# Keys of a cross-attention kernel from seven products of block sums instead of eight

## The chip, the cores and the metric

One core of one Trainium2 chip. The metric is the device time of one execution in microseconds; the times shown are medians over runs of the same kernel. TensorE is called PE here, its weight load PEld, VectorE DVE, ScalarE ACT, GpSimd POOL, and SyncE's DMA queue SP.

## The reference, cut to what matters

A first attention (1x1 convolutions `theta`, `phi` and `g`, a product without softmax, a convolution back, batch norm, residual) turns x [8, 256, 512], with ctx [8, 256, 512], into the rows that enter two layers of cross-attention with 16 heads of 128, and an MLP. Both layers take keys and values from the same context:

```python
def _cross_attention(q_in, kv_in, wq, bq, wk, bk, wv, bv, wo, bo, bias_k, bias_v):
    qh = (q_in @ wq + bq).reshape(b, q_len, H, K)
    kh = (kv_in @ wk + bk).reshape(b, t, H, K)
    vh = (kv_in @ wv + bv).reshape(b, t, H, K)
    kh = jnp.concatenate([kh, jnp.broadcast_to(bias_k, (b, 1, H, K))], axis=1)
    vh = jnp.concatenate([vh, jnp.broadcast_to(bias_v, (b, 1, H, K))], axis=1)
    logits = jnp.einsum('bqhk,bthk->bhqt', qh, kh) / scale
    weights = jax.nn.softmax(logits, axis=-1)
    ctx = jnp.einsum('bhqt,bthk->bqhk', weights, vh).reshape(b, q_len, H * K)
    return ctx @ wo + bo
```

The change concerns `kv_in @ wk`: 2048 context tokens by 512 features, times 512 by 2048 weights, for each of two layers.

## The kernel before, in words

Every large product is made of two parts. An operand is split into a high part (rounded to fp32r) and a low part (what the rounding left), and `product` issues three matmuls for each chunk of 128 features: high by high, high by low, low by high. A high part is one copy or activation, a low part is one subtraction: ACT and DVE make them for activations, POOL for weights (`halve`: a cast, then a subtraction that waits for it).

The front of the kernel computes all keys and values and stores them to DRAM (`kd`, `vd`); behind it, 64 steps load them back, do the attention, and the MLP follows. The front has 8 groups (`GROUPS`), each of four heads. A group has 16 key units (one head by one chunk of 512 tokens, 12 matmuls of 512 columns: 4 chunks of features, 3 each) and 16 value units (one tile of 128 tokens by four heads, 12 matmuls too). The order of all work is written out by hand in `front_order`, and each engine walks the same list. A unit takes one of four PSUM banks (`U`, `RING` = 4) in turn; `take` waits until the unit four before has been read.

A key unit is read from PSUM twice: ACT writes the high part with the bias into one of four slots of `stage` (L791), DVE the low part (L983), and SP stores the slot. A value unit is read once by DVE, which adds the bias row `vb` (L991) into `tmp`; ACT writes the high part from it (L798), DVE the low part (L994), both of whose inputs lie in SBUF.

POOL splits each group's key weights into `wks` while the values of the group before are made, and its value weights into `wvs` while its keys are made (L458 the cast, L461 the subtraction, L476 `vb`). `wvs` is one buffer: it is overwritten only when the last value unit of the group before has been read.

The context is turned by PE (L710) chunk by chunk into `cT`, beside the keys of group 0. The first attention (`first_attention`: pg, M, th, WM, wy for each of eight batches, plain fp32 matmuls, L715 to L726) is spread over the value units of groups 0 and 1 by `L0_PARTS`. In the last group, `JOINT` lays the first normalised rows (`Z`), queries (`q`) and logits (`L`) between the value units. POOL's `normalise` (L522) feeds `Z`, and `add_bias` (L530) adds the output bias to x.

## Time and profile before

| | |
|---|---|
| median of 3 runs | 2396.48 us (2395.93 to 2400.75) |
| profiled execution | 2382.3 us, span 2380.4 us |
| PE busy | 2345.2 us (99% of the span), 12304 matmuls |
| DVE, ACT, POOL busy | 1322.3, 1141.5, 464.6 us |
| DMA | 331.83 MB, 139 GB/s over the span |

Busy time of PE is the union of matmuls whose modelled ends overlap, so the mean duration of one is longer than the distance between two starts. The span is from the first to the last instruction; the profiled execution's time is 1.9 us longer than it.

### The profile page before, as it was taken

How to read it: one execution, taken by the hardware profiler on the slowest of the kernel's cores; microseconds unless marked ns; L12 is line 12 of the kernel's file. 1: busy time of each engine (PE TensorE's matmuls, PEld its weight loads, DVE VectorE, ACT ScalarE, POOL GpSimd, SP SyncE). 2: the span in 40 equal slices, each digit the busy share in tenths (PEclk: the TensorE clock that was granted, in tenths of full speed). 3: DMA queues.
4: the chain of work that ended last, by engine and by line, in shares of the span. 5: the costliest groups of instructions: out<-in, count | busy, mean ns of one | idle time of the engine just before them, and what ended most of it. 6: DMA issues, size and time to landing. Idle time of an engine off the chain costs nothing.

```text
span 2380.4 us, 32423 instructions
## 1 busy us (share of the span) xinstructions
PE 2345.2 (99%) x12304; PEld 1993.2 (84%) x12304; DVE 1322.3 (56%) x2328; ACT 1141.5 (48%) x2717; POOL 464.6 (20%) x280
## 2 busy tenths in 40 slices
PE   8999999999999999999999989999999999999999
PEld 7777788888888788888888878888888887788887
DVE  4444453454454666666666676666666666634433
ACT  3222222222223676666666677666666667322222
POOL 2111121121133610111101253111101115611110
PEclk9999999999999999999999999999999999999999
DMA  7454565665666433433334323333333331100001
GB/s 274 166 190 168 186 221 206 242 219 213 238 221 231 169 116 129 141 128 132 116 126 141 127 87 125 129 136 125 131 125 127 140 124 37 45 19 27 27 1 71
DMA packets 142168, 331.83 MB, mean 139 GB/s; under 512 B 8896, under 2 KB 74944, under 8 KB 125632
## 3 DMA queue, kind: packets, MB, share of 16 engines
q1 hardware_dynamic: 141296, 329.68, 39.5%
q8 instruction: 99, 1.62, 0.3%
q14 instruction: 53, 0.43, 0.1%
q10 hardware_dynamic: 720, 0.10, 0.0%
HBM read 190.81 MB, written 138.94 MB: 139 GB/s over the span
## 4 chain that ended last, share of the span: by engine, by line
PE 90%; ACT 4%; DVE 4%; issue 1%; POOL 0%; DMA 0%; ACTq 0%; DVEq 0%; POOLq 0%
PE U L576 23%; PE U L578 23%; PE U L577 23%; PE T L670 4%; PE O L576 2%; PE S L578 2%; PE O L578 2%; PE O L577 2%; PE S L577 2%; PE S L576 2%; DVE hT L999 1%; ACT aff L809 1%; DVE gT L1009 1%; ACT probs L850 1%; ACT hT L812 1%
## 5 line engine op out<-in xcount | busy, mean ns | idle before, releaser
L1018 DVE TENSOR_TENSOR x<-x,U 128x512 f32<-128x512 f32 x384 | 261.0, 683 | 79.9 <-PE U L578 77.5
L842 ACT ACTIVATE probs<-S,nm 128x257 f32<-128x257 f32 x512 | 237.7, 476 | 30.9 <-DVE nm L1026 30.9
L1026 DVE TENSOR_REDUCE nm<-S 128x2 f32<-128x514 f32 x256 | 177.3, 693 | 123.4 <-PE S L578 119.6
L860 ACT ACTIVATE PT<-T 128x512 fp32r<-128x512 f32 x256 | 152.5, 596 | 172.6 <-PE T L670 172.2
L850 ACT ACTIVATE probs<-probs,rs 128x256 f32<-128x256 f32 x512 | 230.1, 500 | 1.4 <-DVE rs L1030 1.1
L798 ACT ACTIVATE stage<-tmp 128x512 fp32r<-128x512 f32 x128 | 80.9, 632 | 308.8 <-DVE tmp L991 308.8
L576 PE MATMUL U<-wos,oT 128*128 128x512 f32 x512 | 213.0, 416 | 0.8 <-DVE oT L1041 0.8
L791 ACT ACTIVATE stage<-U,hc 128x512 fp32r<-128x512 f32 x128 | 88.3, 689 | 259.5 <-PE U L578 259.5
L983 DVE SCALAR_TENSOR_TENSOR stage<-U,hc,stage 128x512 fp32r<-128x512 f32 x128 | 96.1, 751 | 206.5 <-ACT stage L791 206.4
L576 PE MATMUL U<-wvs,cT 128*128 128x512 f32 x512 | 206.1, 403 | 0.0
L458 POOL CAST wos<-raw 128x1024 fp32r<-128x1024 f32 x20 | 20.8, 1039 | 941.8 <-PE U L578 941.8
L576 PE MATMUL U<-cT,wks 128*128 128x512 f32 x512 | 201.7, 394 | 2.1 <-DVE cT L961 2.1
L1041 DVE SCALAR_TENSOR_TENSOR oT<-O,hc,oT 128x256 fp32r<-128x256 f32 x256 | 123.8, 484 | 142.7 <-ACT oT L869 142.7
L578 PE MATMUL U<-wos,oT 128*128 128x512 f32 x512 | 201.9, 394 | 0.0
L577 PE MATMUL U<-wos,oT 128*128 128x512 f32 x512 | 200.9, 392 | 0.0
L577 PE MATMUL U<-cT,wks 128*128 128x512 f32 x512 | 199.9, 390 | 0.0
L578 PE MATMUL U<-cT,wks 128*128 128x512 f32 x512 | 199.8, 390 | 0.0
L578 PE MATMUL U<-wvs,cT 128*128 128x512 f32 x512 | 199.6, 390 | 0.0
L577 PE MATMUL U<-wvs,cT 128*128 128x512 f32 x512 | 199.5, 390 | 0.0
L1034 DVE TENSOR_TENSOR PT<-T,PT 128x512 fp32r<-128x512 f32 x256 | 175.5, 685 | 41.8 <-ACT PT L860 41.8
L869 ACT ACTIVATE oT<-O,hc 128x256 fp32r<-128x256 f32 x256 | 121.1, 473 | 125.5 <-PE O L578 125.3
L670 PE MATMUL T<-ident,probs 128*128 128x128 f32 x1024 | 154.8, 273 | 14.2 <-ACT probs L850 14.1
(166 smaller groups left out, 5804.5 us busy)
## 6 DMA issues: line engine op xcount, KB each, us to landing
kd<-stage SPq DMA_DIRECT2D x128, 516.0 KB, 3.1
kb<-kd SPq DMA_DIRECT2D x64, 1032.0 KB, 4.8
vd<-stage SPq DMA_DIRECT2D x128, 512.0 KB, 3.2
vb<-vd SPq DMA_DIRECT2D x64, 1024.0 KB, 5.0
raw<-wa SPq DMA_DIRECT2D x24, 512.0 KB, 5.8
raw<-wb SPq DMA_DIRECT2D x24, 512.0 KB, 5.9
raw<-wk SPq DMA_DIRECT2D x16, 512.0 KB, 5.9
raw<-wv SPq DMA_DIRECT2D x16, 512.0 KB, 5.7
```

The lines of the kernel that those rows point to most:

```text
L576: pe.matmul(o, lhs[0], rhs[0], start=start, stop=False)
L577: pe.matmul(o, lhs[0], rhs[1], start=False, stop=False)
L578: return pe.matmul(o, lhs[1], rhs[0], start=False, stop=stop)
L670: mm = pe.transpose(T[:, at_:at_ + P], probs[:, J % 2, qt, tt * P:tt * P + P], ident[:])
L842: ins = act.activation(probs[:, r, qt, 0:257], S[:, qt, 0:257], ACT.Exp, bias=nm[:, r, qt:qt + 1], scale=-1.0, accum_out=sums[:, r, qt:qt ...
L850: ins = act.activation(probs[:, r, qt, 0:256], probs[:, r, qt, 0:256], ACT.Copy, scale=rs[:, r, qt:qt + 1])
L860: act.activation(PT[:, J % 2, 0, :], T[:], ACT.Copy).then_inc(pt_hi, 1)
L869: act.activation(oT[:, 0, h, b * 256:b * 256 + 256], O[:, 0:256], ACT.Identity, bias=hc[:, 3, at_:at_ + 1]).then_inc(o_hi, 1)
L1018: dve.tensor_tensor(x[:, tile, :], x[:, tile, :], bank(what, s, t), ALU.add).then_inc(free, 1)
L1026: dve.tensor_reduce(nm[:, J % 2, :], S[:, :, 0:257], AX.X, ALU.min).then_inc(least, 1)
L1034: dve.tensor_tensor(PT[:, J % 2, 1, :], T[:], f(PT[:, J % 2, 0, :]), ALU.subtract).then_inc(pt, 1)
L1041: dve.scalar_tensor_tensor(out=oT[:, 1, h, to], in0=O[:, 0:256], scalar=hc[:, 3, at_:at_ + 1], in1=f(oT[:, 0, h, to]), op0=ALU.add, op1=AL ...
```

## The change

A pair of heads (left and right 128 columns of a weight tile) and a pair of 512-token chunks form a 2 by 2 block of keys, and the 512 features are taken as two halves of 256. Eight block products become seven (Winograd's variant of Strassen's scheme): P1, P6, P2, P7, P5, P3, P4, each of 6 matmuls, with sums of weight blocks S1 to S4 and of context blocks T1 to T4 as operands. The four key blocks C11, C22, C12, C21 come from sums of the products.

- The front runs in two passes (`PAIRS`) of 1024 tokens; a pass has 8 rounds, a round two quads (`i` = 0, 1; seven products each) and 8 value units. Each weight is loaded and split once a pass.
- Context: `plain` holds the two parts of one pass's blocks, `tform` those of T1 to T4. The blocks are turned in an opening ahead of each pass; for the second pass its plain parts are made by turning again (`cT`) beside the values of round 7. T1 to T4 are formed by DVE from PSUM, their high parts by ACT, their low parts by POOL (`forms_lo`).
- Weights: POOL forms S1 to S4 for each quad and splits all seven left operands into `wks`, which holds one quad: the cast of product k waits for product k of the quad before. PE waits for `k_form` product by product.
- Results: ACT copies P1 to SBUF; DVE makes seven sums (`products`), four of them keys in `z`. ACT writes the high part and the bias columns, DVE the low part from `z` and `stage`.
- The first attention is gathered in the two openings (`opening`), with a doubled `xb`. Block sums of weights `ks` and raw value weights `rawv` share memory with its buffers.
- At the join, DVE normalises two tiles of each of the first two chunks, and `JOINT` is folded into 8 value units. `hT` is four tensors, one for each chunk.

```diff
+B11, B12, B22, B21 = range(4)
+T1, T2, T3, T4 = range(4)
+T_ORDER = (T1, T3, T2, T4)
+P1, P6, P2, P7, P5, P3, P4 = range(7)
+C11, C22, C12, C21 = range(4)
+KEY_OF = {C11: (0, 0), C12: (0, 1), C21: (1, 0), C22: (1, 1)}
+
+
+LAST_SUM = {P6: 1, P2: 2, P7: 3, P5: 5, P3: 6, P4: 7}
+MADE_BY = {C11: 2, C22: 5, C12: 6, C21: 7}
+
+
+LAST_FORM = ({B11: 2, B12: 4, B22: 6, B21: 8}, {B11: 1, B12: 2, B22: 3, B21: 4})
+FORMED_BY = ({T1: 1, T3: 3, T2: 5, T4: 7}, {T1: 1, T3: 2, T2: 3, T4: 4})
+
...
+def opening(p):
+
+    def blocks(i):
+        return [("B", p, i, blk) for blk in range(4)]
+
+    b = 4 * p
+    out = [("pg", b, 0), ("pg", b, 1)] + blocks(0)
+    for b in range(4 * p, 4 * p + 4):
+        more = b + 1 < 4 * p + 4
+        out += [("M", b, 0)] + ([("pg", b + 1, 0)] if more else [])
+        out += blocks(1) if b == 4 * p else []
+        out += [("th", b, 0), ("WM", b, 0)] + ([("pg", b + 1, 1)] if more else [])
+        out += [("wy", b, 0), ("wy", b, 1)]
+    return out
 
...
-            if e == GROUPS - 1:
+    out = []
+    for r in range(ROUNDS):
+        if r % GROUPS == 0:
+            out += opening(r // GROUPS)
+        for i in range(2):
+            for k in range(7):
+                out.append(("K", r, i, k))
+                if k == P6 and i == 1:
+                    out.append(("C", r, 0, C21))
+                elif k == P7:
+                    out.append(("C", r, i, C11))
+                elif k == P3:
+                    out.append(("C", r, i, C22))
+                elif k == P4:
+                    out.append(("C", r, i, C12))
+        out.append(("C", r, 1, C21))
+        for t in range(PAIR_TILES):
+            out.append(("V", r, t))
+            if r == GROUPS - 1:
+                out.append(("cT", 2 + t // CH, t % CH))
+            if r == ROUNDS - 1:
                 out += JOINT.get(t, [])
     return out
...
+        tform = at(r + 32768, 32768, ("tform0", [2, 4, 2, 512], F32R)) + at(r, 32768, ("tform1", [2, 4, 2, 512], F32R))
+        hT = at(r, 65536, *((f"hT{c}", [2, CH, 512], F32R) for c in range(CHUNKS)))
         raw = [sb(f"raw{i}", [CH, 256]) for i in range(2)]
...
+        (wks,) = at(r, 16384, ("wks", [2, 7, 2, P], F32R))
         wqs, wos = at(r, 16384, ("wqs", [2, CH, 256], F32R), ("wos", [2, 2, D], F32R))
...
+            def load_value_weights(r):
+
+                e = r % GROUPS
                 for i in range(2):
-                    load(i, 2 * e + 1, wv[2 * e + i])
-                if e:
-                    sp.wait_ge(vb_ready, e)
+                    if e == 0:
+                        sp.wait_ge(z_x, TILES // 2 * (r // GROUPS + 1))
+                    else:
+                        sp.wait_ge(split_v[i], r)
+                    sp.dma_start(rawv[i][:], wv[2 * e + i]).then_inc(rawv_in[i], 16)
+                if r:
+                    sp.wait_ge(vb_ready, r)
+                if e == 0:
+                    sp.wait_ge(t_lo, 8 * (r // GROUPS + 1))
                 sp.dma_start(raw_vb[:].rearrange("p a b n -> p (a b) n"),
...
+            def forms_lo(p, i):
+
+                for n, form in enumerate(T_ORDER):
+                    pool.wait_ge(t_hi, 8 * p + 4 * i + n + 1)
+                    pool.tensor_tensor(tform[p][:, 1, form, i, :], temp(i, form), f(tform[p][:, 0, form, i, :]),
+                                       ALU.subtract).then_inc(t_lo, 1)
+
+            def keys(r, i):
+
+                n = quad(r, i)
+                a11, a12 = raw[i][:, 0:2, 0:P], raw[i][:, 2:4, 0:P]
+                a21, a22 = raw[i][:, 0:2, P:2 * P], raw[i][:, 2:4, P:2 * P]
+                s1, s2, s3, s4 = (ks[:, k] for k in range(4))
+                pool.wait_ge(raw_in[i], 16 * (r + 1))
+                if n:
+                    pool.wait_ge(k_form, 7 * n)
+                if r % GROUPS == 0 and i == 1:
+                    pool.wait_ge(z_x, TILES // 2 * (r // GROUPS + 1))
+                pool.tensor_tensor(s1, a21, a22, ALU.add).then_inc(s_form, 1)
+                pool.tensor_tensor(s3, a11, a21, ALU.subtract).then_inc(s_form, 1)
+                pool.wait_ge(s_form, 4 * n + 1)
+                pool.tensor_tensor(s2, s1, a11, ALU.subtract).then_inc(s_form, 1)
+                pool.wait_ge(s_form, 4 * n + 3)
+                pool.tensor_tensor(s4, a12, s2, ALU.subtract).then_inc(s_form, 1)
+                sources = {P1: a11, P6: s2, P2: a12, P7: s3, P5: s1, P3: s4, P4: a22}
+                first = casts["done"]
+                for k in range(8):
+                    if k < 7:
+                        if n:
+                            pool.wait_ge(unit, UNIT["K", (n - 1) // 2, (n - 1) % 2, k] + 1)
+                        if k == P3:
+                            pool.wait_ge(s_form, 4 * n + 4)
+                        pool.tensor_copy(wks[:, 0, k], sources[k]).then_inc(hi_part, 1)
+                    if k:
+                        pool.wait_ge(hi_part, first + k)
+                        pool.tensor_tensor(wks[:, 1, k - 1], sources[k - 1], f(wks[:, 0, k - 1]), ALU.subtract).then_inc(k_form, 1)
+                casts["done"] += 7
+
+            def values(r, i):
+
+                if r:
+                    pool.wait_ge(free, FREE["V", r - 1, PAIR_TILES - 1] + 1)
+                if i == 0:
+                    pool.wait_ge(vrow_in, 16 * (r + 1))
+                    pool.tensor_tensor(vb[:], raw_vb[:, :, 0, :], raw_vb[:, :, 1, :], ALU.subtract).then_inc(vb_ready, 1)
+                to = slice(i * 256, i * 256 + 256)
+                pool.wait_ge(rawv_in[i], 16 * (r + 1))
+                pool.tensor_copy(wvs[:, 0, :, to], rawv[i][:]).then_inc(hi_part, 1)
+                casts["done"] += 1
+                pool.wait_ge(hi_part, casts["done"])
+                pool.tensor_tensor(wvs[:, 1, :, to], rawv[i][:], f(wvs[:, 0, :, to]), ALU.subtract).then_inc(split_v[i], 1)
...
+            keys(0, 0)
+            for r in range(ROUNDS):
+                if r % GROUPS == 0:
+                    for i in range(2):
+                        forms_lo(r // GROUPS, i)
+                    keys(r, 1)
+                    values(r, 0)
+                else:
+                    values(r, 0)
+                    keys(r, 1)
+                values(r, 1)
+                if r + 1 < ROUNDS:
...
+            def keys(r, i, k):
+                p = r // GROUPS
+                pe.wait_ge(k_form, 7 * quad(r, i) + k + 1)
+                if (r % GROUPS, i, k) == (0, 0, P1):
+                    if p == 0:
+                        pe.wait_ge(formed, formed_before(1, 0))
+                    else:
+                        pe.wait_ge(free, FREE["cT", CHUNKS - 1, CH - 1] + 1)
+                    pe.wait_ge(t_lo, 8 * (p + 1))
+                o = take("K", r, i, k)
+                for j in range(2):
+                    if k == P1:
+                        own = parts(plain[p], j, slice(0, 512))
+                    elif k == P2:
+                        own = parts(plain[p], 2 + j, slice(0, 512))
+                    elif k == P3:
+                        own = parts(plain[p], 2 + j, slice(512, 1024))
+                    else:
+                        own = parts(tform[p], {P4: T4, P5: T1, P6: T2, P7: T3}[k], j)
+                    mm = product(o, parts(wks, k, j), own, j == 0, j == 1)
                 mm.then_inc(unit, 1)
 
...
+            def first_product(r, i):
+                n = quad(r, i)
+                act.wait_ge(unit, UNIT["K", r, i, P1] + 1)
+                if n % (2 * GROUPS):
+                    act.wait_ge(summed, 7 * (n - 1) + 2)
+                else:
+                    act.wait_ge(z_x, TILES // 2 * (r // GROUPS + 1))
+                act.activation(aff[:, 1, :], bank("K", r, i, P1), ACT.Copy).then_inc(copied, 1)
+
+            def keys(r, i, o):
+                n = KV["C", r, i, o]
+                h = KEY_OF[o][0]
+                at_ = head_of(r, i, h)
                 slot_free(n)
-                at_ = 4 * e + h
-                act.activation(key_slot(0, n), by_batch(bank("K", e, c, h)), ACT.Identity,
-                               bias=hc[:, 1, at_:at_ + 1]).then_inc(hi, 1)
-
...
+            def products(r, i, k):
+
+                n = 7 * quad(r, i)
+                o = bank("K", r, i, k)
+                u2, u3, u4, first = us[:, 0, :], us[:, 1, :], aff[:, 0, :], aff[:, 1, :]
+
+                def key(to, left, right, op):
+                    at_ = head_of(r, i, KEY_OF[to][0])
+                    if quad(r, i) % (2 * GROUPS):
+                        dve.wait_ge(staged, KV["C", (quad(r, i) - 1) // 2, (quad(r, i) - 1) % 2, to] + 1)
+                    dve.scalar_tensor_tensor(out=z[:, to, :], in0=left, scalar=hc[:, 1, at_:at_ + 1], in1=right,
+                                             op0=ALU.add, op1=op).then_inc(summed, 1)
+
+                if k == P1:
+                    if quad(r, i) % (2 * GROUPS) == 0:
+                        dve.wait_ge(t_lo, 8 * (r // GROUPS + 1))
+                        dve.wait_ge(z_x, TILES // 2 * (r // GROUPS + 1))
+                    return
+                dve.wait_ge(unit, UNIT["K", r, i, k] + 1)
+                if k == P6:
+                    if n:
+                        dve.wait_ge(summed, n)
+                    dve.wait_ge(copied, COPIED["K", r, i, P1] + 1)
+                    dve.tensor_tensor(u2, first, o, ALU.add).then_inc(summed, 1)
+                elif k == P2:
+                    key(C11, first, o, ALU.add)
+                elif k == P7:
+                    dve.wait_ge(summed, n + 1)
+                    dve.tensor_tensor(u3, u2, o, ALU.add).then_inc(summed, 1)
+                elif k == P5:
+                    dve.tensor_tensor(u4, u2, o, ALU.add).then_inc(summed, 1)
+                    dve.wait_ge(summed, n + 3)
+                    key(C22, u3, o, ALU.add)
+                elif k == P3:
+                    dve.wait_ge(summed, n + 4)
+                    key(C12, u4, o, ALU.add)
+                else:
+                    key(C21, u3, o, ALU.subtract)
+
+            def keys(r, i, o):
+                n = KV["C", r, i, o]
+                dve.wait_ge(hi, HI["C", r, i, o] + 1)
+                dve.tensor_tensor(key_slot(1, n), by_batch(z[:, o, :]), f(key_slot(0, n)), ALU.subtract).then_inc(staged, 1)
+
```

## Rows read from the trace of the kernel before

**Rows 1.** The page: busy time by engine; the chain that ended last.
```profile
PE 2345.2 (99%) x12304; PEld 1993.2 (84%) x12304; DVE 1322.3 (56%) x2328; ACT 1141.5 (48%) x2717; POOL 464.6 (20%) x280
...
PE 90%; ACT 4%; DVE 4%; issue 1%; POOL 0%; DMA 0%; ACTq 0%; DVEq 0%; POOLq 0%
PE U L576 23%; PE U L578 23%; PE U L577 23%; PE T L670 4%; PE O L576 2%; PE S L578 2%; PE O L578 2%; PE O L577 2%; PE S L577 2%; PE S L576 2%; DVE hT L999 1%; ACT aff L809 1%; DVE gT L1009 1%; ACT probs L850 1%; ACT hT L812 1%
```

**Rows 2.** Windows: stretch, length, busy time by engine, granted clock, DMA share, GB/s.
```profile
12.44:794.98 782.54, 781.18 (x3461) 638.43 (x3461) 365.45 (x610) 207.74 (x332) 161.92 (x94) 1.00 0.59 210
...
435.54:522.58 87.04, 87.04 (x386) 72.10 (x385) 38.79 (x64) 21.16 (x33) 15.63 (x10) 1.00 0.63 224
```

**Rows 3.** Timeline, PE, the first key matmuls of a group: start, length.
```profile
521.61 0.39 PE L576 MATMUL U<-cT,wks 128*128 128x512 f32 x1
...
521.83 0.39 PE L577 MATMUL U<-cT,wks 128*128 128x512 f32 x1
```

**Rows 4.** Timeline, PE: turned context, first attention, and what follows.
```profile
20.49 0.60 PE L710 MATMUL T<-ident,x 128*128 128x128 f32 x4
...
20.85 0.48 PE L576 MATMUL U<-cT,wks 128*128 128x512 f32 x1
...
66.00 3.61 PE L715 MATMUL S<-wpg,x 128*128 128x256 f32 x16
...
75.96 1.88 PE L719 MATMUL O<-xb,wth 128*128 128x512 f32 x4
```

**Rows 5.** Groups of DVE: busy us, mean ns of one, idle before them.
```profile
L994 DVE TENSOR_TENSOR stage<-tmp,stage 128x512 fp32r<-128x512 f32 x128 | 100.5, 785 | 99.6 <-ACT stage L798 99.6
L983 DVE SCALAR_TENSOR_TENSOR stage<-U,hc,stage 128x512 fp32r<-128x512 f32 x128 | 96.1, 751 | 206.5 <-ACT stage L791 206.4
```

**Rows 6.** Timeline, POOL, one group's value weights.
```profile
522.58 1.29 POOL L476 TENSOR_TENSOR vb<-raw_vb 128x512 f32<-128x512 f32 x1 [36.97 <-DVE tmp L991]
523.81 1.51 POOL L458 CAST wvs<-raw 128x1024 fp32r<-128x1024 f32 x1
525.39 2.40 POOL L461 TENSOR_TENSOR wvs<-raw,wvs 128x1024 fp32r<-128x1024 f32 x1
527.73 1.05 POOL L458 CAST wvs<-raw 128x1024 fp32r<-128x1024 f32 x1
```

**Rows 7.** Timeline, DVE and POOL side by side at the join.
```profile
743.66 0.84 DVE L994 TENSOR_TENSOR stage<-tmp,stage 128x512 fp32r<-128x512 f32 x1 [0.77 <-ACT stage L798]
...
744.04 2.73 POOL L461 TENSOR_TENSOR wos<-raw,wos 128x1024 fp32r<-128x1024 f32 x1
...
763.12 8.26 POOL L522 TENSOR_SCALAR z<-x,mv,rstd 128x512 f32<-128x512 f32 x4 [14.92 <-PE U L613]
...
764.45 0.69 DVE L994 TENSOR_TENSOR stage<-tmp,stage 128x512 fp32r<-128x512 f32 x1 [0.77 <-ACT stage L798]
...
771.36 5.04 POOL L530 TENSOR_TENSOR x<-x,brow 128x512 f32<-128x512 f32 x4
...
772.72 4.25 DVE L994 TENSOR_TENSOR stage<-tmp,stage 128x512 fp32r<-128x512 f32 x1 [0.77 <-ACT stage L798]
...
776.36 1.51 POOL L513 TENSOR_TENSOR rstd<-vpe,minus_half 128x4 f32<-128x4 f32 x1
```

**Rows 8.** Groups of POOL: the cast of 1024 columns, and normalise.
```profile
L458 POOL CAST wks<-raw 128x1024 fp32r<-128x1024 f32 x16 | 16.6, 1038 | 244.2 <-PE U L578 237.7 <-DMA raw<-wk 6.6
...
L522 POOL TENSOR_SCALAR z<-x,mv,rstd 128x512 f32<-128x512 f32 x44 | 92.3, 2109 | 28.8 <-PE U L613 28.1 <-POOL rstd L513 0.4 <-PE U L578 0.2
```

**Rows 9.** DMA issues: queue, count, size, us to landing.
```profile
raw_vb<-vrow SPq DMA_DIRECT2D x8, 512.0 KB, 6.4
```

**Rows 10.** Timeline, PE, the start of the kernel.
```profile
6.77 1.94 PE L710 MATMUL S<-ident,x 128*128 128x128 f32 x8 [6.77 <-DMA x<-ctx_in]
...
12.47 0.77 PE L576 MATMUL U<-cT,wks 128*128 128x512 f32 x1 [2.06 <-DVE cT L961]
...
13.89 0.63 PE L576 MATMUL U<-cT,wks 128*128 128x512 f32 x1
14.31 0.63 PE L577 MATMUL U<-cT,wks 128*128 128x512 f32 x1
```

**Rows 11.** The end of the steps: a window, and PE's timeline in it.
```profile
2010.00:2020.00 10.00, 8.47 (x40) 7.26 (x41) 6.88 (x16) 8.12 (x14) 5.82 (x4) 0.83 0.00 0
...
2011.53 0.66 PE L670 MATMUL T<-ident,probs 128*128 128x128 f32 x4 [2.85 <-ACT probs L850]
...
2012.77 0.63 PE L576 MATMUL U<-wos,oT 128*128 128x512 f32 x1
2013.19 0.63 PE L577 MATMUL U<-wos,oT 128*128 128x512 f32 x1
```

More of the change, by code:

```diff
@@ L55 @@
 RING = 4
[L67 to L90 removed]
+PAIRS = CHUNKS // 2
@@ L581, in parts, with await_bank @@
                 return t[(slice(None), 0, *ix)], t[(slice(None), 1, *ix)]
+            def await_bank(*name):
+                what, *a = name
+                if what == "K" and a[2] == P1:
+                    pe.wait_ge(copied, COPIED[name] + 1)
+                elif what == "K":
+                    pe.wait_ge(summed, 7 * quad(a[0], a[1]) + LAST_SUM[a[2]])
+                elif what == "B":
+                    pe.wait_ge(formed, formed_before(a[0], a[1]) + LAST_FORM[a[0]][a[2]])
+                else:
+                    pe.wait_ge(free, FREE[name] + 1)
@@ L583, in take, with blocks @@
             def take(*name):
                 if UNIT[name] >= RING:
-                    pe.wait_ge(free, UNIT[name] - RING + 1)
+                    await_bank(*UNITS[UNIT[name] - RING])
                 return bank(*name)
-            def keys(e, c, h):
-                if c == 0 and h % 2 == 0:
-                    pe.wait_ge(split[h // 2], 2 * e + 1)
-                o = take("K", e, c, h)
-                for ch in range(CH):
-                    if e == 0 and h == 0:
-                        pe.wait_ge(z_free_v, l0_taken(("cT", c, ch), TO_V))
-                    mm = product(o, parts(wks, ch, slice(h * P, h * P + P)), parts(cT, ch, columns(c)), ch == 0, ch == CH - 1)
+            def blocks(p, i, blk):
+                c, ch = {B11: (0, 0), B12: (1, 0), B22: (1, 2), B21: (0, 2)}[blk]
+                turned_context(take("B", p, i, blk), 2 * p + c, ch + i).then_inc(unit, 1)
@@ L597, in keys, with values @@
                 mm.then_inc(unit, 1)
-            def values(e, t):
+            def values(r, t):
                 if t == 0:
                     for i in range(2):
-                        pe.wait_ge(split[i], 2 * e + 2)
-                o = take("V", e, t)
+                        pe.wait_ge(split_v[i], r + 1)
+                o = take("V", r, t)
                 for ch in range(CH):
-                    mm = product(o, parts(cT, ch, slice(t * P, t * P + P)), parts(wvs, ch, slice(0, 512)), ch == 0, ch == CH - 1)
+                    mm = product(o, parts(plain[r // GROUPS], ch, slice(t * P, t * P + P)), parts(wvs, ch, slice(0, 512)), ch == 0, ch == CH - 1)
@@ L707, in first_attention @@
                 o = l0_bank(*name)
-                if what == "cT":
-                    for t in range(4):
-                        mm = pe.transpose(o[:, t * P:t * P + P], x[:, 4 * b + t, part * P:part * P + P], ident[:])
-                elif what == "pg":
+                if what == "pg":
                     for i in range(2):
@@ L732, in _ @@
                     keys(*a)
+                elif what == "B":
+                    blocks(*a)
+                elif what == "cT":
+                    turned_context(take("cT", *a), *a).then_inc(unit, 1)
                 elif what == "V":
@@ L764, in first_attention @@
                 act.wait_ge(z_unit, L0[name] + 1)
-                if what == "cT":
-                    act.activation(cT[:, 0, part, columns(b)], o, ACT.Copy).then_inc(z_hi, 1)
-                elif what == "th":
+                if what == "th":
                     act.activation(th[:], o, ACT.Identity, bias=thb_s[:, 0:1]).then_inc(z_free_a, 1)
@@ L958, in first_attention @@
                 o = l0_bank(*name)
[L959 to L962 removed]
+                if what == "pg":
+                    if b == 4 and part == 0:
+                        dve.wait_ge(split_v[0], GROUPS)
                     dve.wait_ge(z_unit, L0[name] + 1)
```

388 lines of the change are left out of this document (238 added, 150 removed).

## The prediction

> **What bounds the kernel now.** I read the page's busy line and chain first: PE is busy 99% of the span, 90% of the chain that ended last is PE, and the three matmul lines of `product` carry it [rows 1]. So this is a TensorE kernel, and what the change is worth is read in its first stage. The windows say where that is: the front runs from 12.44 to 794.98 us with PE busy for all but 1.4 us of it, and one steady group (16 key units, 16 value units) takes 87.04 us with POOL busy only 15.6 us [rows 2]. 87.04 us over 384 matmuls is 0.2267 us each, which is also the distance between two starts [rows 3]; the 390 ns that the group view gives as the mean of one are overlapping ends and must not be used as a price. The reader should hold on to two things: a matmul saved is worth 0.227 us, and the side engines are nearly free now, so that their work costs nothing until a group gets so short that one of them is the longer chain.
>
> **What PE saves.** 128 key units of 12 matmuls (1536) become 32 quads of 7 products of 6 (1344): 192 less, 192 x 0.2267 = **-43.5 us**. The context is transposed again for the block sums: 96 transposes of 128 columns instead of 64. Four of them hold PE 0.36 us (20.49 to 20.85) [rows 4], so 32 x 0.09 = **+2.9**. The matmuls of the first attention are the same; they only move.
>
> **What the side engines get.** A quad gives PE 42 x 0.2267 = 9.52 us. DVE: seven sums from PSUM (at most 0.75 each) and four low parts whose two inputs are both in SBUF (0.785), 8.4 us [rows 5]: under 9.52, off the path, but close. Its bias-column copies go to ACT, which has room (5 copies of a bank and 4 tiny ones a quad). The SP queue gets 16 more key weight and 16 more value weight loads; each is issued a V stage or more ahead of its use, except in rounds 0 and 8 (below). The zero cost of these rests on that cover.
>
> **POOL is what I cost in full.** wks holds one quad, so product k's weights can be written only after product k of the quad before. wvs holds one round, so it can be written only after the last value tile, and V's first tile waits for both halves. In `values(r,0)`, `keys(r,1)`, `values(r,1)` POOL must therefore run all between the end of one V stage and the start of the next, while PE has only the K stage, 2 x 9.52 = 19.04 us. Before, one V weight split stood beside a 43.5 us K stage. The chain, from the first key matmul:
> - last tile's copy on DVE, then POOL starts: 521.61 to 522.58, 0.97 [rows 3, 6];
> - vb, and the first half of wvs: 522.58 to 527.73, 5.15 [rows 6];
> - four block sums of 256 columns. POOL's two-input instruction follows its like after 1.25 us at 512 columns (four in 5.00) and after 2.34 at 1024 (525.39 to 527.73) [rows 6, 7]: 2.13 ns a column and 0.16 fixed, so 0.70 at 256. 4 x 0.70 + 0.16 for two waits = 2.96;
> - seven casts and seven subtractions. The cast of 1024 columns takes 1.04 [rows 8]; a quarter is 0.26, and with POOL's 0.1 to 0.2 fixed I take 0.36. 7 x (0.36 + 0.70) = 7.42;
> - the second half of wvs: 1.05 + 0.08 + 2.40 = 3.53 [rows 6]; 0.10 for the hand-over to PE.
> Sum 20.13, already 1.1 over PE's 19.04.
>
> **Collisions.** A DVE instruction with both inputs in SBUF and a POOL cast or two-input instruction exclude each other. At 743.66 the low part comes during a cast, takes 0.84 instead of 0.69, and the POOL subtraction behind it 2.73 instead of 2.40; the cast at 523.81 took 1.51 instead of 1.04 [rows 6, 7]. A collision so costs POOL 0.33 to 0.47. The low parts of keys were read from PSUM and never collided; now eight a round read z and stage, and POOL is busy throughout. One collision is in the 5.15 already; seven more at 0.4 are 2.8 us. Chain **22.9, 3.9 us over PE**: about 1.3 as a wait of quad 1's first product (its weights are ready at 0.97 + 5.15 + 2.96 + 2 x 0.36 + 0.70 + 0.4 = 10.9, PE is there at 9.52), the rest before V. 14 rounds x 3.9 = **+54.6**.
> Bounds per round: with quarter prices (0.26, 0.60) and no collision the chain is 0.97 + 4.68 + 2.56 + 6.02 + 3.53 + 0.10 = 17.9, no stall; with 0.45 and 0.80 and ten collisions of 0.5 it is about 27, a stall of 8.
> In rounds 0 and 8 vb's row is asked for only after C11 of quad 0 is stored (about 7.5 us into K) behind two 0.45 us issues and lands 6.4 later [rows 9], so POOL starts vb at about 15.5; 15.5 + 5.15 + 3.53 + 0.1 = 24.3, 5.2 over: **+10.4** for both.
>
> **Openings and join.** The first attention, spread over V tiles before, now runs in two openings. PE's work in it (16 recorded pg matmuls 3.4 us, th 1.7, wy) [rows 4] is laid between its own hand-overs, so that only the last batch's ones are bare. A hand-over over two engines costs 0.97 [rows 3]. One bare per opening: 2 us; if all five of each batch were bare, 8 x 5 x 0.97 = 39. At the start PE now waits for pgw and pgb too, but before it lost 6.77 and then 2.06 us, and its first matmuls ran at 0.42 us apart [rows 10]; I take zero, bound -3 to +5. At the join, Z(0,2) follows Z(0,1) within some 7 us while POOL's four `normalise` instructions take 8.4 [rows 8]: +2. Together **+4**, bounds -3 and +46.
>
> **The clock.** After PE idled 2.85 us before 2011.53, matmuls stood 0.42 us apart from 2012.77 and the granted clock of that 10 us stretch is 0.83, that is 1.7 us lost at the lower level (1.2 GHz) [rows 11]. My waits before V are 2.6 us, nearly as long. I take a third of the rounds: 5 x 1.7 = **+8**; bounds 0 and 27.
>
> **Sum**: -43.5 + 2.9 + 54.6 + 10.4 + 4 + 8 = **+36.4 us** on the profiled execution's 2382.3 (span 2380.4 and 1.9 around it). The median shown, 2396.48, is 14.2 above that execution; added to it: **2433 us**.
>
> **The rivals.**
> A. *POOL keeps up* (the other side). If pieces of 256 columns cost a quarter and collisions hide in POOL's own gaps, only rounds 0 and 8 wait: -43.5 + 2.9 + 10.4 = -30.2, 2366; it holds down to a stall of 2.1 us a round (2.1 x 14 + 10.4 + 2.9 = 43), where the gain is gone. For it: POOL's fixed part at 256 columns is extrapolated, the cast's from one size only. Against: without a single collision I already stand 1.1 over. 2366 to 2391.
> B. *DVE starves and takes the bound.* Beside four POOL two-input instructions in a row the low part at 772.72 took 4.25 us [rows 7]. If low parts in the K stage each wait for about a cast and a subtraction (1.06), a quad costs DVE 8.4 + 4 x 1.06 = 12.6 against 9.52; the four PSUM banks then run out, 3.1 us a quad, 6.2 a round: -43.5 + 2.9 + 87 + 10.4 + 8 + 4 = +69, 2465. Against: DVE did get in between a cast and the instruction behind it.
> The Trainium skill's "SBUF — State Buffer" (SBUF: two separate sides) calls this an exclusive lock, held for a whole instruction, for every GpSimd instruction that reads SBUF. This trace agrees for casts and two-input ones, but not for the scalar one: beside four `normalise` instructions at 763.12 the low part took its plain 0.69 [rows 7]. By the page the join's DVE work would wait for POOL too, some 2 us more; by the row it does not.
> C. *Openings bare*: +39 instead of +2 with my other terms: 2470.
> D. *Nothing measurable*: stall near 2.1, 2392 to 2401.
>
> **Chances and range.** Forecast 0.50 (its own range 2403 to 2460), A 0.26, B 0.11, C 0.06, D 0.07. A change of over 0.2% (4.8 us) is about what a measurement of this kernel tells from none. Faster 0.26, same 0.07, slower 0.67. Range 2369 to 2472: it takes in nearly all of A and of B, as their bounds ask, and leaves out the high ends.
>
> **What the profile will show.** Right: 1344 key matmuls; rounds of about 45 us where 40.9 is PE alone; PE's longest waits are for POOL's wks and wvs, POOL busy some 75% of a round; wks pieces at 0.70 and 0.36; casts and subtractions stretched beside DVE's low parts. Wrong if PE waits on wks and wvs are under 2 us a round (A), if they name DVE sums (B), or if the two openings show PE idle for tens of us (C).

## The result, and the profile after

The kernel with the seven products takes 2436.31 us (2429.64 to 2438.72) against 2396.2 us (2384.62 to 2400.75) on the same chip: ratio 1.0162, 95% interval 1.0130 to 1.0194. It is slower by 40 us; 2433 was forecast, with 2369 to 2472 as range. The profiled executions stand further apart, 2438.72 against 2382.3, that is 56.4 us. Keep both differences in mind: experiment 12 bears on what lies between them.

The page of the profile, in the lines that answer to [rows 1]:

```profile
span 2436.9 us, 33484 instructions
...
PE 2330.1 (96%) x12144; PEld 1965.9 (81%) x12144; DVE 1526.5 (63%) x2444; ACT 1177.4 (48%) x2897; POOL 883.4 (36%) x876
...
PE 79%; POOL 7%; DVE 5%; ACT 5%; issue 2%; DMA 1%; SPq 0%; DVEq 0%; POOLq 0%; ACTq 0%
```

160 matmuls fewer (192 products saved, 32 transposes more), and POOL on the critical chain with 7%, where it had none. What PE waited for (in all, times, longest):

```profile
PE U L739 <- POOL wks L612: 24.6, 14, 1.8
PE U L739 <- issue: 23.1, 15, 6.2
PE T L867 <- ACT probs L1077: 18.8, 17, 6.7
PE S L908 <- DMA pgb_s<-pgb: 10.4, 1, 10.4
PE U L810 <- DVE hT L1310: 7.4, 1, 7.4
PE O L919 <- ACT wm L967: 3.8, 2, 3.5
```

The row "issue" names nobody: it is in the main the wait ahead of the value stage, and POOL's rows below show that the value weights' last low part has just ended there. One steady round, the window of 44 us that answers to [rows 2] (a group of before is two such rounds), and two windows behind the long waits of rounds 0 and 8:

```profile
509.00:553.00 44.00, 41.43 (x181) 33.52 (x180) 31.23 (x38) 11.93 (x26) 33.65 (x41) 1.00 0.73 251
85.40:109.30 23.90, 23.80 (x96) 19.54 (x97) 10.55 (x15) 4.43 (x7) 11.41 (x18) 0.91 0.76 257
485.40:509.00 23.60, 23.60 (x97) 19.34 (x98) 10.61 (x15) 4.43 (x7) 15.24 (x22) 0.92 0.76 262
```

POOL is busy 33.65 of 44 us, 76%. PE has 180 matmuls in 180 x 0.2267 = 40.8 us, and the timeline shows where the other 3.3 go. First POOL (answers to [rows 6]), then PE's two waits in that round:

```profile
509.93 1.29 POOL L621 TENSOR_TENSOR vb<-raw_vb 128x512 f32<-128x512 f32 x1 [9.21 <-DVE tmp L1302]
511.16 1.51 POOL L624 CAST wvs<-rawv 128x1024 fp32r<-128x1024 f32 x1
...
515.11 0.74 POOL L595 TENSOR_TENSOR ks<-raw 128x256 f32<-128x256 f32 x1
515.81 1.20 POOL L596 TENSOR_TENSOR ks<-raw 128x256 f32<-128x256 f32 x1
...
518.45 0.86 POOL L609 CAST wks<-raw 128x256 fp32r<-128x256 f32 x1
519.26 0.40 POOL L609 CAST wks<-ks 128x256 fp32r<-128x256 f32 x1
519.63 0.72 POOL L612 TENSOR_TENSOR wks<-raw,wks 128x256 fp32r<-128x256 f32 x1
...
527.12 1.50 POOL L624 CAST wvs<-rawv 128x1024 fp32r<-128x1024 f32 x1
528.71 2.38 POOL L627 TENSOR_TENSOR wvs<-rawv,wvs 128x1024 fp32r<-128x1024 f32 x1
...
554.01 1.29 POOL L621 TENSOR_TENSOR vb<-raw_vb 128x512 f32<-128x512 f32 x1 [10.11 <-DVE tmp L1302]
```

```profile
520.40 0.50 PE L739 MATMUL U<-plain,wks 128*128 128x512 f32 x1 [1.75 <-POOL wks L612]
...
531.19 0.47 PE L739 MATMUL U<-wvs,plain 128*128 128x512 f32 x1 [0.81 <-issue]
```

The reader sees a chain without a gap from 509.93 to 531.05, 21.1 us of POOL for 19.04 us of PE; vb of the next round starts 44.08 us later. Pieces of 256 columns run undisturbed at 0.40 (cast) and 0.72 to 0.75 (two inputs), and some stand at 0.86 and 1.20, each 0.46 longer. Over the whole kernel (mean ns in the last column but one):

```profile
L612 POOL TENSOR_TENSOR wks<-ks,wks 128x256 fp32r<-128x256 f32 x128 | 97.7, 763 | 0.0
...
L609 POOL CAST wks<-raw 128x256 fp32r<-128x256 f32 x96 | 68.1, 710 | 0.0
L609 POOL CAST wks<-ks 128x256 fp32r<-128x256 f32 x128 | 58.0, 453 | 0.0
```

Then the join and the first steps behind it, PE, DVE and POOL:

```profile
838.44 0.90 PE L867 MATMUL T<-ident,probs 128*128 128x128 f32 x3 [6.67 <-ACT probs L1077]
...
865.52 14.90 POOL L682 TENSOR_TENSOR x<-x,brow 128x512 f32<-128x512 f32 x12
...
870.81 11.13 DVE L1310 TENSOR_TENSOR hT<-aff,hT 128x512 fp32r<-128x512 f32 x1 [1.65 <-ACT hT L1039]
...
882.00 1.11 PE L810 MATMUL U<-ident,z 128*128 128x128 f32 x4 [7.44 <-DVE hT L1310]
```

A DVE instruction that otherwise takes 0.69 us was held 11.13, and PE waited 7.44 for it. It ended at 881.94, so by its plain 0.69 it ran from about 881.25: the string of twelve additions was over by then (880.42), and so, but for the last 0.15 us, was the cast behind it (880.36 to 881.40). This document calls that the hold. Two DVE instructions with one input in PSUM passed beside the same additions in their plain time (866.27, 0.69 and 867.03, 0.69). The kernel before has the same twelve additions; in its profiled execution the DVE instruction was through after 1.42 us, and POOL's string is the longer one:

```profile
821.61 16.31 POOL L530 TENSOR_TENSOR x<-x,brow 128x512 f32<-128x512 f32 x12
```

```profile
825.74 1.42 DVE L999 TENSOR_TENSOR hT<-aff,hT 128x512 fp32r<-128x512 f32 x1 [1.64 <-ACT hT L812]
```

**The ledger of the profiled executions.** At the first T matmul of the steps the kernel after is 838.44 - 794.98 = 43.5 us late (before's mark is the end of the front in [rows 2]). In that stand -43.5 + 2.9 for PE's work, 14 x 3.3 = 46.2 for the steady rounds, 12.3 for the waits of rounds 0 and 8 (6.20 and 6.11), and a rest of 25.6. Two windows split the rest, after and before:

```profile
0.00:838.44 838.44, 763.83 (x3317) 609.57 (x3317) 566.64 (x733) 247.96 (x518) 587.88 (x700) 0.98 0.66 226
```

```profile
0.00:794.98 794.98, 784.83 (x3477) 641.71 (x3477) 369.54 (x615) 211.32 (x338) 166.93 (x103) 1.00 0.60 211
```

PE stood still 74.6 us, against 10.2 before. A steady round has 44.00 - 41.43 = 2.57 of that, 14 of them 36.0; with these, the 12.3 and before's 10.2 taken off, 16.2 us of waits are left for the 25.6. The start is 3.7 later (10.44 against 6.77), wm in the opening costs 3.50, probs at the join 6.67 (1.33 before), the others are small. The other 9.4 us are matmuls that took longer. The granted clock was below 1.00 in several stretches behind waits: 0.83 between 20 and 40 us, and 0.91 and 0.92 behind the long ones, which is 2 us of 23.9 each. From 838.44 to the end the kernel loses another 13.0 us, 7.1 of them in waits, where the 7.44 above is the largest, and 5.9 in matmuls that took longer: in the 18 us behind the hold the granted clock was 0.73.

```profile
882.00:900.00 18.00, 15.88 (x76) 13.47 (x77) 11.03 (x21) 13.06 (x32) 2.16 (x1) 0.73 0.11 32
```

### The profile page after: what moved, and what is told of

It reads as the page before. It is cut to its first block, busy times and chain, and to the rows that moved or that the text cites. A ratio compares the mean times of both kernels' runs of the same rounds, so it can differ in the third digit from the quotient of the medians.

```text
span 2436.9 us, 33484 instructions
## 1 busy us (share of the span) xinstructions
PE 2330.1 (96%) x12144; PEld 1965.9 (81%) x12144; DVE 1526.5 (63%) x2444; ACT 1177.4 (48%) x2897; POOL 883.4 (36%) x876
## 4 chain that ended last, share of the span: by engine, by line
PE 79%; POOL 7%; DVE 5%; ACT 5%; issue 2%; DMA 1%; SPq 0%; DVEq 0%; POOLq 0%; ACTq 0%
PE U L739 20%; PE U L741 19%; PE U L740 19%; PE T L867 4%; PE O L739 2%; PE O L741 2%; PE S L741 2%; PE O L740 2%; PE S L739 2%; PE S L740 2%; POOL wvs L627 2%; DVE hT L1310 2%; ACT aff L1036 1%; POOL wvs L624 1%; ACT probs L1077 1%
## 5 line engine op out<-in xcount | busy, mean ns | idle before, releaser
L739 PE MATMUL U<-wvs,plain 128*128 128x512 f32 x512 | 203.3, 397 | 23.2 <-issue 23.1
L741 PE MATMUL U<-wvs,plain 128*128 128x512 f32 x512 | 200.8, 392 | 0.0
L740 PE MATMUL U<-wvs,plain 128*128 128x512 f32 x512 | 200.8, 392 | 0.0
L1305 DVE TENSOR_TENSOR stage<-tmp,stage 128x512 fp32r<-128x512 f32 x128 | 114.9, 898 | 98.8 <-ACT stage L1024 98.8
L1018 ACT ACTIVATE stage<-z 128x512 fp32r<-128x512 f32 x128 | 81.0, 633 | 191.1 <-DVE z L1263 190.7
L1055 ACT ACTIVATE tmp<-U,f1c 128x512 f32<-128x512 f32 x64 | 44.0, 688 | 247.4 <-PE U L741 247.4
L1320 DVE TENSOR_TENSOR gT<-tmp,gT 128x512 fp32r<-128x512 f32 x64 | 58.4, 913 | 163.8 <-ACT gT L1063 163.8
L739 PE MATMUL U<-hT,wqs 128*128 128x512 f32 x384 | 156.8, 408 | 1.5 <-DVE hT L1310 1.5
```

What stands on the lines that cost most here:

```text
L739: pe.matmul(o, lhs[0], rhs[0], start=start, stop=False)
L740: pe.matmul(o, lhs[0], rhs[1], start=False, stop=False)
L741: return pe.matmul(o, lhs[1], rhs[0], start=False, stop=stop)
```

## The experiments

Each ratio is to the kernel before as it ran beside the experiment: 2394.32 us for experiments 1 to 4, 2395.74 for 5 to 8, 2396.4 for 9 to 11, and 2395.97 for 12. Differences to 2436.31 join measurements that were not made side by side, so a few us of them may be the measurement.

**1. The value weights' casts go to ACT.** POOL keeps the low part.

```diff
-                pool.tensor_copy(wvs[:, 0, :, to], rawv[i][:]).then_inc(hi_part, 1)
-                casts["done"] += 1
-                pool.wait_ge(hi_part, casts["done"])
+                pool.wait_ge(v_hi, 2 * r + i + 1)
...
+                    act.activation(wvs[:, 0, :, i * 256:i * 256 + 256], rawv[i][:], ACT.Copy).then_inc(v_hi, 1)
```

> The two casts of the value weights move from POOL to ACT; nothing else changes. Theory (between two V stages the POOL chain, 22.2 us, is longer than PE's 19.04): POOL loses two casts of 1.51 us and their 0.08 us waits, gains about 0.7 us of waiting for ACT, so the chain falls to 19.8 us, a round from 44.1 to about 41.6, and the kernel by 14 x 2.5 plus about 4 in rounds 0 and 8, from 2436 to about 2397 us. Rival (DVE's sums, or the openings and the join, hold the time): rounds stay at 44.1 and the kernel at 2436.

2402.54 us (2399.36 to 2406.06), ratio 1.0039 (1.0026 to 1.0051): 34 us come back, 5 less than forecast; rounds are 41.97 us where 41.6 was forecast, and 14 x 0.37 is that 5. The longest wait for wks is 0.7 us, and "issue" is left with two waits, those of rounds 0 and 8:

```profile
PE U L737 <- POOL wks L612: 9.8, 14, 0.7
...
PE U L737 <- issue: 7.2, 2, 3.6
```

So two casts a round shorten the stall as if they stood on the path, which they do.

**2. No collisions with DVE in the K stage.** DVE's key low part takes its second input from PSUM. The low parts of the keys are then not the true ones; size and count of all instructions stay.

```diff
-  by_batch(z[:, o, :]), f(key_slot(0, n)), ALU.subtract)
+  by_batch(z[:, o, :]), by_batch(S[:, 0, :]), ALU.subtract)
```

> DVE's low part of each key block subtracts a PSUM bank instead of the slot's high part in SBUF (the stored low parts are therefore not the true ones); the instruction count, shapes and waits stay. Theory (collisions are part of the stall): about five collisions of 0.46 us a round go, casts on POOL return from 0.86 to 0.40 us, rounds fall from 44.1 to about 41.8, the kernel to about 2402 us; the DVE low part of keys falls from 1189 to about 690 ns. Rival (POOL's own instructions alone make the chain): rounds above 43.5, kernel above 2430.

2405.68 us (2404.55 to 2407.3), ratio 1.0053 (1.0033 to 1.0073), some 4 us above the forecast. Rounds are 41.95 us, 2.15 less than 44.1, so the collisions were 30 us of the 46.2. DVE's key low part takes 685 ns in the mean where it took 1189. In the group of casts the stretched ones are gone, 397 ns where 710 stood:

```profile
L609 POOL CAST wks<-raw 128x256 fp32r<-128x256 f32 x96 | 38.1, 397 | 0.0
```

**3. One product more on PE.** P4 of each quad is multiplied out twice, the second time over the first, so PE again has 1536 key matmuls.

```diff
+                    if k == P4 and j == 1:
+                        for j in range(2):
+                            own = parts(tform[p], T4, j)
+                            mm = product(o, parts(wks, k, j), own, j == 0, j == 1)
```

> Product P4 of each quad is computed twice, so PE again does 1536 key matmuls, 43.5 us more than in the changed kernel. Theory (POOL paces the K stage): PE's K stage of 21.8 us is still within POOL's 22.2, so the kernel costs 0 to 5 us more, 2436 to 2441. Rival (PE paces, the waits are elsewhere): about 43 us more, 2480.

2440.87 us (2440.19 to 2441.12), ratio 1.0198 (1.0175 to 1.0222). Matmuls worth 192 x 0.2267 = 43.5 us cost 4.6 us, as the theory had it. A round is 44.22 us instead of 44.1: POOL sets its length, and the matmuls that PE saves only turn into waits.

**4. The join respaced.** The rows of the second normalised chunk enter the value stage one value unit earlier, and the first probabilities stand alone behind the last one.

```diff
-         4: [("q", 0, 0, 0), ("q", 0, 0, 1)], 5: [("q", 0, 1, 0), ("q", 0, 1, 1)],
-         6: [("Z", 0, 1, 0), ("L", 0), ("Z", 0, 1, 1)], 7: [("Z", 0, 1, 2), ("Z", 0, 1, 3), ("X", 0)]}
+         4: [("q", 0, 0, 0), ("q", 0, 0, 1)], 5: [("Z", 0, 1, 0), ("q", 0, 1, 0), ("q", 0, 1, 1), ("Z", 0, 1, 1)],
+         6: [("Z", 0, 1, 2), ("L", 0), ("Z", 0, 1, 3)], 7: [("X", 0)]}
```

> Only the order of the join changes: the second chunk's normalised rows are turned from value unit 5 on, not from unit 6 on, and the division of the first probabilities stands alone behind unit 7. Theory (the join's 6.7 us wait comes from rows and probabilities queued together on ACT and DVE behind the last value unit): PE's first T follows the last value unit within 3 us, the clock does not fall there, and the kernel is 8 to 12 us faster than 2436, 2424 to 2428. Rival (the wait is set by when the second chunk is normalised): 2434 to 2438.

2438.5 us (2436.85 to 2439.65), ratio 1.0189 (1.0169 to 1.0209): nothing gained, half a microsecond above the rival's range. The 6.7 us wait becomes 4.28, but one of 2.23 us now stands ahead of the logits (832.79), where 0.29 stood (830.82): 6.5 us in all against 7.0. The wait has moved and not gone, and the 7.4 us wait for hT stays.

**5. The next query weights back between normalise(0, 2) and normalise(0, 3).**

```diff
             normalise(0, 2)
+            queries(1)
             normalise(0, 3)
             for c in range(1, CHUNKS):
                 add_bias(0, c)
-            queries(1)
```

> The weights of queries(1) are prepared by POOL between normalise(0, 2) and normalise(0, 3), as in the kernel before, not behind the twelve bias adds; nothing else moves. Theory (the 7.4 us PE wait at the first attention step is DVE's hold behind the twelve additions): the additions stay twelve in a row, so the hold and the wait stay, and the time is 2433 to 2440 us. Rival (it is the place of the next query weights in POOL's order that makes the join late): 2424 to 2431.

2437.23 us (2429.33 to 2442.73), ratio 1.0166 (1.0120 to 1.0212): no change, as the theory had it, and the hold is still there, 10.17 us:

```profile
868.68 10.17 DVE L1310 TENSOR_TENSOR hT<-aff,hT 128x512 fp32r<-128x512 f32 x1 [1.64 <-ACT hT L1039]
```

Here no cast follows the twelve additions. They end at 878.30, the DVE instruction at 878.85, and the hold is about one cast of 1.04 us shorter than the 11.13.

**6. A break between the bias adds of layer 0.**

```diff
                     pool.tensor_tensor(x[:, t, :], x[:, t, :], brow[:], ALU.add).then_inc(ln_bias, 1)
+                    if n == 0:
+                        pool.tensor_copy(scratch[:, t, :], minus_half[:])
```

> A four-column POOL copy into a tile that nothing reads is put behind each of the 16 bias adds of layer 0, so that twelve two-input POOL additions no longer follow one another without a break. Nothing is left out. Theory (the DVE high part that took 11.13 us behind POOL's 12 additions waits for a break in POOL's string, and the 7.4 us PE wait and part of the clock fall behind it are its price): the DVE instruction falls to 1 to 3 us, the PE wait at the first attention step goes, 7 to 14 us come off: 2422 to 2429 us. Rival (POOL's additions slow DVE by their traffic, whatever stands between them, or the break is too short to let DVE in): the DVE instruction stays near 11 us and the time at 2434 to 2439.

2431.27 us (2430.35 to 2435.87), ratio 1.0148 (1.0106 to 1.0189). The median is 5 to 6 us below the versions with the hold, but its range overlaps theirs (2429.64 to 2438.72, and 2429.33 to 2442.73 in experiment 5), and it lies between the two forecasts. So the time does not decide; the trace decides for the theory. The DVE instruction that was held has its 0.69 us, and no wait of PE on hT over 1 us is left:

```profile
870.67 0.69 DVE L1313 TENSOR_TENSOR hT<-aff,hT 128x512 fp32r<-128x512 f32 x1 [1.65 <-ACT hT L1042]
```

```profile
869.50 1.30 POOL L683 TENSOR_TENSOR x<-x,brow 128x512 f32<-128x512 f32 x1
870.72 0.69 POOL L685 COPY scratch<-minus_half 128x4 f32<-128x4 f32 x1
871.37 1.30 POOL L683 TENSOR_TENSOR x<-x,brow 128x512 f32<-128x512 f32 x1
```

DVE starts at 870.67, while the fourth addition runs, and POOL's tiny copy behind it takes 0.69 instead of 0.20: POOL now waits for DVE there, half a microsecond instead of eleven.

**7. The sums of a round's second quad, a value stage early.**

```diff
                 if r + 1 < ROUNDS:
                     keys(r + 1, 0)
+                    if (r + 1) % GROUPS:
+                        weight_sums(r + 1, 1)
```

(`weight_sums` holds the wait for raw and the four sums of `keys`, which keeps them for the other quads.)

> POOL forms the four sums S1 to S4 of a round's second key quad at the end of the value stage before, and no longer between the value weights and the first key part; all products stay. Theory (the 3.3 us stall of a round is POOL's chain from the first value part to the last, 22.2 us against 19.0 us of key products, and the sums are 3.7 us of it): the chain falls to 18.5 us, the wait before V and the one before P1 vanish in 14 of 16 rounds, rounds fall from 44.1 to 41.0 to 41.5 us, and the time by 36 to 44 us: 2393 to 2401 us. Rival (the chain is bound by the key products that free each weight slot, so that POOL only waits longer elsewhere, or the sums now delay the high and low parts of the round's first quad): rounds stay at 43 us or more, 2420 us or more.

2402.73 us (2394.85 to 2409.59), ratio 1.0020 (0.9991 to 1.0048). 34 us come back, 2 less than the low end of the forecast. No execution stands near the median: five lie between 2394.85 and 2398.77, as forecast, and five between 2406.7 and 2409.59. The profiled one (2396.43) is of the shorter five; what the longer ones lose no trace shows. Rounds are 41.04 us, with no wait for wks among the large ones, so the mechanism is the one expected. The hold behind twelve additions is in this trace too, 11.10 us, as it was in the kernel that this version starts from.

```profile
530.65 1.29 POOL L630 TENSOR_TENSOR vb<-raw_vb 128x512 f32<-128x512 f32 x1 [6.68 <-DVE tmp L1313]
571.69 1.29 POOL L630 TENSOR_TENSOR vb<-raw_vb 128x512 f32<-128x512 f32 x1 [6.18 <-DVE tmp L1313]
```

**8. Experiments 1, 6 and 7 together.**

> Together: the value weights' casts on ACT, the four sums of a round's second quad a stage early, and the four-column copies between the bias adds. Nothing is left out. If the key stalls, which casts on ACT alone took to 41.95 us a round, and the hold of DVE behind 12 additions are separate costs, they add up: 2402.5 (casts on ACT alone) less some 5 to 10 for the rest of the stalls less 7 to 14 for the copies gives 2379 to 2391 us, faster than the kernel before. If the stalls hide one another or the copies do nothing: 2396 to 2403.

2375.95 us (2370.42 to 2387.24), ratio 0.9917 (0.9887 to 0.9947), below the low end forecast, and faster than the kernel before. A round is now 40.80 us, PE's own 180 matmuls:

```profile
522.23 1.29 POOL L631 TENSOR_TENSOR vb<-raw_vb 128x512 f32<-128x512 f32 x1 [8.55 <-DVE tmp L1325]
563.03 1.29 POOL L631 TENSOR_TENSOR vb<-raw_vb 128x512 f32<-128x512 f32 x1 [8.55 <-DVE tmp L1325]
```

The hold is gone from layer 0, and stands in layer 1, whose additions had no break:

```profile
1426.96 14.90 POOL L690 TENSOR_TENSOR x<-x,brow 128x512 f32<-128x512 f32 x12
```

```profile
1432.01 11.38 DVE L1333 TENSOR_TENSOR hT<-aff,hT 128x512 fp32r<-128x512 f32 x1 [1.64 <-ACT hT L1058]
```

**9 to 11. The same with breaks in every layer; without 1; with 4.** The edit is that of experiment 6 without its `if n == 0`.

> The three changes together (value-weight casts on ACT, the second quad's sums a stage early, four-column copies between the bias adds), now with the copies behind the adds of every layer, 48 in all. Nothing is left out. Theory (in the run with copies in layer 0 alone the hold came back at layer 1's twelve adds, a PE wait of 7.7 us at 1443 us, since only those adds had no break): no PE wait on hT over 1 us, 5 to 9 us less than that run's 2375.95: 2367 to 2372 us. Rival (the hold at layer 1 was chance of phase and costs little outside the profiled run): within 0.2% of 2376.

> As the three together, but the value weights' casts stay on POOL. If POOL's chain is short enough once the sums are gone from it (rounds of 41.0 us in the run of that alone), this is within 5 us of the version with casts on ACT; rival: the casts' 2.6 us a round still show in rounds 0 and 8 and in some 0.2 us of every other round: 5 to 10 us slower.

> The three together, with the respaced join on top (the first layer's normalised chunk enters a step earlier). Theory: alone it changed nothing (2438.5 against 2436.3) because other waits took the place of the 2.4 us it removed, so here too: within 3 us of the version without it. Rival: the 7.4 us hold that followed had hidden its gain, and it now gives 4 to 8 us.

With breaks everywhere 2373.88 us (2371.06 to 2378.19), ratio 0.9904 (0.9884 to 0.9923); no PE wait on hT over 1 us is left, but the gain over experiment 8 is 2 us, within what can be told apart, where the theory wanted 5 to 9: by the time its rival was right, and the hold of layer 1 cost little outside the profiled execution, which was the longest of eight. Its slowest execution is 9 us below that of experiment 8. With the casts back on POOL 2386.11 us (2381.63 to 2388.75), ratio 0.9955 (0.9940 to 0.9970), 12 us slower, more than either view had: the two long waits are 12.9 us in all instead of 7.2, and its rounds 41.16 us instead of 40.80, 14 x 0.36 = 5.0. With the join respaced 2374.09 us (2370.66 to 2378.3), ratio 0.9906 (0.9886 to 0.9927): nothing, as the theory had it, even with the hold out of its way.

**12. The kernel before, with breaks between its 48 bias adds.** The same one line, in the kernel before.

> The kernel before, with a four-column POOL copy behind each of its 48 bias adds and nothing else changed; nothing is left out. In the profile shown of the kernel before no DVE instruction was held over 4.3 us. Theory (the hold is a matter of phase that this kernel rarely meets): the same time within 0.2%, 2392 to 2401 us. Rival (its slower executions, up to 2400 and more, hold DVE behind twelve adds, as the kernel after does): 4 to 12 us faster, so that the copies, and not the seven products, would own much of the lead of the combined version.

2383.36 us (2380.55 to 2386.23, 12 executions), where the kernel before has 2395.97 (2382.99 to 2409.59, 17 executions): ratio 0.9949 (0.9928 to 0.9970). The rival was right, with 12.6 us against its 4 to 12. The copies do work that nobody needs, and the spread falls from 27 to 6 us, around what had been the kernel's shortest time. Without them the 17 executions stand in three clusters some 10 us apart: five between 2382.99 and 2388.23, nine between 2394.43 and 2400.57, three between 2403.93 and 2409.59. That would fit none, one or two holds in an execution, but no trace of one from the upper two exists. The profiled execution of before, 2382.3 us, was of the lowest, and the copies do not shorten that one (2383.28 profiled with them).

## Why the prediction was right, and where it was not

**PE's saving (-43.5, +2.9)** holds: 192 key matmuls less, and experiment 3 shows that giving them back costs 4.6 us. The saving was real and PE could not use it.

**POOL's chain (+54.6)** was the step that carried the forecast. Forecast 22.9 us from the first key matmul to the first value matmul; measured 0.97 (109.31 to 110.28 us in round 1) + 21.1 + 0.14 = 22.2. The pieces were costed at 0.36 and 0.70 from start to start; they stand at 0.37 and 0.68 apart (519.26 to 519.63, 523.19 to 523.87), and the wait of quad 1's first product was to be 1.3 and is 1.75. That it exceeds PE's 19.04 even undisturbed is what experiment 2 shows: 1.15 us a round of stall are left without the collisions. Without the sums (experiment 7) 0.24 are left. The term came to 3.3 us a round, 46.2 instead of 54.6.

**Collisions (7 more at 0.4, with one in the 5.15)**: in the round shown six instructions are stretched (both value casts, three key casts, one sum), 4 x 0.46 + 2 x 0.47 = 2.8 us, where eight at 0.4 gave 3.2. Taking them away took 2.15 us off a round.

**Rounds 0 and 8 (+10.4)**: waits of 6.20 and 6.11 us, 12.3. POOL starts vb 16.85 and 16.40 us after the first key matmul, where 15.5 was taken; the parts named for it (7.5, two issues of 0.45, 6.4) add up to 14.8 only. The two rawv issues held the queue for 2.0 us (67.95 to 69.97) and not 0.9.

**Openings, join and clock (+4 and +8)** are the terms that were mis-sized. In the profiled execution they hold 25.6 us up to the first T matmul and 13.0 behind it, 38.6, instead of 12; the 7.44 us wait of the hold and the clock behind it are in the 13.0. I had placed +2 at the join for Z(0,2). PE's only wait there for POOL's z is 1.35 us, ahead of the first normalised rows (802.88); the large one is that of the first attention chain itself, 6.67 us for probs, with no value tile left to cover it. Neither experiment 4 nor 11 gained by moving Z, which speaks against POOL's normalise as the cause. The start is 3.7 us later where I took zero: PE's first instruction waits 10.44 us for pgb. And the clock fell elsewhere than I had it: I gave +8 to waits before V in a third of the steady rounds, and those waits are 0.8 us with the clock at 1.00; it fell behind the waits of the opening, of rounds 0 and 8, of the join and of the hold.

**The step I did not have is the hold.** I had seen its small form, 4.25 us of DVE beside four additions [rows 7], and used it only for rival B in the key stage, where casts stand between two-input instructions. Beside twelve additions it is 11.13 us. The kernel before most likely has it as well: breaks gain 12.6 us there. That would also explain, though no trace of one of its longer executions shows it, the 14.2 us by which its median stood over its profiled execution, a number that I carried along as if it were noise. By the profiled executions the change costs 56.4 us and the forecast was +36.4; by the medians it costs 40.1, since before's median most likely contains holds too. Without that the forecast would have looked 20 us too low. It was right in its main mechanism, and the closeness of 2433 to 2436 is in part luck: two errors that cancel.

The Trainium skill's "SBUF — State Buffer" (SBUF: two separate sides) calls the port pair of VectorE and GpSimd an exclusive lock for a whole instruction. By that rule a DVE instruction would wait for one POOL instruction (1.25 us here). The trace agrees only in part: it waited for all that were left of twelve.

**Rivals.** A (POOL keeps up) fell with the chain of 22.2 us; its stall of under 2.1 us a round is reached only with the edits of experiments 1, 2 and 7 to 11. B (DVE starves) did not happen in the key stage: its low parts there take 1.19 us in the mean (0.785 before [rows 5]), so a meeting costs DVE 0.4 us where this rival needed 1.06, and no PE wait of note names a DVE sum. C (openings bare) fell: the second opening has PE busy 37.12 of 38 us, and the first 42.55 of 49.21.

**What stays open.** Where the 6.7 us at the join could be covered; why DVE got in beside the twelve additions in one kernel and not in the other, when it came some 0.3 to 0.4 us into an addition in both (825.74 and 870.81, by additions 1.25 us apart); and whether the longer executions of the kernel before show the hold where its additions stand, since the profiled one shows none. That the copies bring the 12.6 us is shown by the edit; that they do it by ending holds, and where, is argued from the kernel after.

## What to carry to other kernels

Saving work on the engine that bounds a kernel shortens the stage in which the side engines must finish theirs: add up each side engine's chain between its two fixed points (here from the last read of wvs to its next first read) before counting the saving, collisions with DVE included. A chain like this is mended by moving the part that has no need to be in it: four sums moved one stage ahead gave 34 us of the 40, and with the casts on ACT, which was busy 11.93 of 44 us in a round, and breaks in POOL's strings the seven products run at 0.9904 (0.9884 to 0.9923) of the kernel before. Measured against the kernel before with the same breaks, 2383.36, the lead of 2373.88 is 9.5 us (0.4%), not 22 (the two were not run side by side, but their ranges, 2371.06 to 2378.19 and 2380.55 to 2386.23, do not meet): apply a side finding to both kernels before crediting the idea.

## What the runs showed of the hardware

- A string of two-input POOL instructions on SBUF can shut out a DVE instruction with two SBUF inputs until the string is over (11.13 us of twelve, 11.38 in another trace, 10.17 in a third), while in the kernel before DVE was through after 1.42 us beside the same twelve. DVE instructions with one input in PSUM were not held (0.69). With a copy of four columns behind each addition, 0.20 us alone and 0.65 to 0.71 when it meets DVE, the `hT` instruction took at most 1.84 us beside them (827.23 in experiment 12's trace). POOL's `normalise`, with one tensor input, did not hold it in [rows 7].
- A cast followed by a two-input instruction did let DVE in: 0.46 us per meeting on pieces of 256 columns.
- In the kernel before, 27 us between the shortest and the longest execution became 6 us with 48 copies that nothing reads. That it was the hold is likely and not shown.
- Behind PE waits of 6.2 and 6.1 us the granted clock of the next 24 us was 0.91 and 0.92, some 2 us lost at the lower level each, and behind the 7.44 us wait 0.73 in 18 us; the 1.75 and 0.8 us waits of a steady round left the clock at 1.00 in its window.
